# Row sums from accumulating exponentials: denominators folded into the softmax shift

## The reference

```python
def attention(q, k, v, wq, wk, wv, wo_w, wo_b):
    qp = rope(einsum('bsd,ed->bse', q, wq))
    kp = rope(einsum('bsd,ed->bse', k, wk))
    vp = einsum('bsd,ed->bse', v, wv)
    scores = einsum('bhnqd,bhnkd->bhnqk', qb, kband) * sqrt(32)
    scores = where(abs(k_pos - q_pos) <= 128, scores, neg)     # a band of keys
    out = einsum('bhnqk,bhnkd->bhnqd', softmax(scores, -1), vband)
    return einsum('bsd,ed->bse', out, wo_w) + wo_b

def ffn(x, W_in, b_in, W_out, b_out):                          # 8-bit weights, 16-bit activations, simulated
    hidden = gelu(quantize_a16(x) @ quantize_w8(W_in) + b_in)
    return quantize_a16(hidden) @ quantize_w8(W_out) + b_out

x = x + attention(layernorm(x), ctx, ctx, wq, wk, wv, wo_w, wo_b)
x = x + ffn(layernorm(x), W_in, b_in, W_out, b_out)
```

## Time and profile before

| | |
|---|---|
| median of 3 runs | 1174.8 us (1173.72 to 1175.84) |
| profiled execution | 1176.49 us, its span 1174.8 us |
| granted TensorE clock, mean | 0.988 |
| TensorE busy | 1135.5 us, 97% |
| VectorE busy | 946.8 us, 81% |
| ScalarE busy | 646.8 us, 55% |
| GpSimd busy | 375.7 us, 32% |

### The profile page before, as it was taken

The page is one execution under the profiler, slowest core; times in us unless marked ns, Lnnn a source line. Parts: engine busy times, 40 slices in busy tenths (PEclk is TensorE's granted clock), DMA queues, the critical chain, the costliest instruction groups (busy, mean ns, idle before and its releaser), DMA issues.

```text
span 1174.8 us, 23540 instructions
## 1 busy us (share of the span) xinstructions
PE 1135.5 (97%) x7928; PEld 766.9 (65%) x7928; DVE 946.8 (81%) x2413; ACT 646.8 (55%) x1033; POOL 375.7 (32%) x540
## 2 busy tenths in 40 slices
PE   6999999999999999999999789999999999999998
PEld 6867887887788788778878464444444444444443
DVE  6879989999999999999998756666666687777776
ACT  5255356436534643563464255555555577777774
POOL 1247337534743663474365230000000021111121
PEclk9989999999999999999999799999999999999999
DMA  8554674566457556646753723555553402676662
GB/s 281 133 150 114 172 221 118 148 184 163 126 175 212 129 137 184 172 123 179 203 139 92 222 65 118 197 196 198 196 196 117 152 1 77 214 232 227 224 216 99
DMA packets 100522, 191.10 MB, mean 163 GB/s; under 512 B 13376, under 2 KB 30912, under 8 KB 100416
## 3 DMA queue, kind: packets, MB, share of 16 engines
q1 hardware_dynamic: 96096, 179.92, 50.9%
q10 hardware_dynamic: 4320, 9.83, 2.8%
HBM read 89.16 MB, written 43.91 MB: 113 GB/s over the span
## 4 chain that ended last, share of the span: by engine, by line
PE 44%; DVE 26%; issue 25%; DMA 2%; ACT 1%; SPq 1%; DVEq 0%; POOL 0%; POOLq 0%; ACTq 0%
PE bank L864 19%; DVE bank L1224 12%; PE bank L642 6%; PE bank L656 5%; PE bank L669 5%; DVE row_max L1224 3%; PE bank L589 3%; PE bank L593 2%; DVE neg_max L1265 2%; DVE roped L1250 2%; DVE rt L1248 2%; DVE rt L1247 1%; DVE neg_max L1229 1%; DVE t_lo L1257 1%; PE bank L608 1%
## 5 line engine op out<-in xcount | busy, mean ns | idle before, releaser
L1224 DVE CUSTOM_DVE_ANT_0 bank<-bank,mask 128x256 f32<-128x256 f32 x512 | 203.5, 453 | 33.9 <-PE bank L608 23.1
L864 PE MATMUL bank<-wout_int,g_hi 128*128 128x512 bf16 x512 | 193.6, 379 | 0.1
L864 PE MATMUL bank<-wout_int,g_lo 128*128 128x512 bf16 x512 | 193.6, 379 | 0.0
L825 PE MATMUL bank<-qT_hi,win_int 128*128 128x512 bf16 x496 | 188.0, 379 | 0.0
L825 PE MATMUL bank<-qT_lo,win_int 128*128 128x512 bf16 x496 | 188.0, 379 | 0.0
L973 ACT ACTIVATE probs<-bank 128x512 f32<-128x512 f32 x256 | 139.0, 599 | 37.0 <-PE bank L642 31.1
L1542 POOL TENSOR_TENSOR k_lo<-roped,k_hi 128x256 fp32r<-128x256 f32 x60 | 55.0, 947 | 263.5 <-ACT k_hi L913 263.5
L1520 DVE TENSOR_TENSOR g_lo<-h_int,g_hi 128x512 f16<-128x512 f32 x128 | 89.1, 696 | 41.3 <-ACT g_hi L1129 37.4
L1565 POOL TENSOR_SCALAR_AFFINE_SELECT probs<-probs 128x256 f32<-128x256 f32 x256 | 107.1, 429 | 35.9 <-ACT probs L973 30.0
L1097 ACT ACTIVATE h_ring<-bank,b_in,g_scale 128x512 f32<-128x512 f32 x96 | 73.1, 779 | 71.2 <-PE bank L825 56.4
L1462 DVE TENSOR_REDUCE hmax<-h_ring 128x512 f32 (+1 forms) x96 | 63.1, 682 | 58.5 <-ACT h_ring L1097 56.4
(11 more groups left out here) (170 smaller groups left out, 2735.0 us busy)
## 6 DMA issues: line engine op xcount, KB each, us to landing
hidden_scratch<-h_ring SPq DMA_DIRECT2D x96, 256.0 KB, 2.1
h_ring<-hidden_scratch SPq DMA_DIRECT2D x96, 256.0 KB, 2.9
k_st<-k_hi SPq DMA_DIRECT2D x128, 128.0 KB, 2.9
q_st<-q_hi SPq DMA_DIRECT2D x128, 128.0 KB, 2.7
xq<-x_scratch SPq DMA_DIRECT2D x16, 1024.0 KB, 6.0
x_ln<-in_x SPq DMA_DIRECT2D x16, 512.0 KB, 6.3
ctx_raw<-in_ctxT SPq DMA_DIRECT2D x16, 512.0 KB, 5.0
k_st<-k_lo SPq DMA_DIRECT2D x64, 128.0 KB, 2.8
```

The source lines that it names most:

```text
L825: mm = pe.matmul(bank[f % 4][:], win_int[:, c, f * P:(f + 1) * P], part[:, par, c], start=c == 0 and part is qT_hi, stop=c == KC - 1 and p ...
L864: return pe.matmul(bank[4 * par + u][:], part[:, f % 4, u * P:(u + 1) * P], wout_int[:, f], start=f == 0 and part is g_hi, stop=f == FC - ...
L1224: dve.tensor_tensor_reduce(sc, sc, mask[:, (1 - qb) * P:(1 - qb) * P + S], 1.0, NEG, ALU.add, ALU.max, row_max[:, qb, n:n + 1]).then_inc(m ...
```

## The change

Scores come out negated: `wq` is scaled by -sqrt(32) when it is split (`wq_scaled`, `wq_rest`), so VectorE takes row minima, and the masked entries are a large positive number. In the first half ScalarE takes, after VectorE's minimum of a head, the exponential of the masked scores in place, with the minimum as bias, and accumulates its row sum: two instructions of 128x256 per head (`row_sums`). After head 15, ScalarE computes the logarithm of all sums and the exponential of its negation (`logs`), and VectorE combines minimum, logarithm and one correction step into the shift rows (`log_sums`, five instructions). With these, the exponential of the second half gives normalised probabilities. The denominators, their inversion, the DMAs, `normalise` and the `pick` matmuls are gone.

A score bank is now free when the sums have read it. Heads 12 and 15 use a third bank (6). The k cast moves from ScalarE to GpSimd (`k_lead`), the ctx cast from ahead of the exponentials to behind the fifth, and GpSimd's four `ctx_lo` to behind bands 10 to 13. Twelve output products stand before the shift transposes, where there were seven.

```diff
-            def row_maxima(b, n):
+            def row_minima(b, n):
                 dve.wait_ge(s_mm, H * b + n + 1)
                 apart(dve)
                 for qb in range(2):
-                    sc = ring[n % 2][:, qb * S:(qb + 1) * S]
-                    dve.tensor_tensor_reduce(sc, sc, mask[...], 1.0, NEG, ALU.add, ALU.max, row_max[:, qb, n:n + 1]).then_inc(max_done, 1)
+                    sc = early[n][:, qb * S:(qb + 1) * S]
+                    dve.tensor_tensor_reduce(sc, sc, mask[...], 1.0, FAR, ALU.add, ALU.min, row_min[:, qb, n:n + 1]).then_inc(min_done, 1)
...
+            def row_sums(b, n):
+                if n == 0:
+                    wait(act, lse_chain, LSE_OPS * b)
+                act.wait_ge(min_done, 2 * (H * b + n + 1))
+                for qb in range(2):
+                    sc = early[n][:, qb * S:(qb + 1) * S]
+                    act.activation(sc, sc, ACT.Exp, scale=-1.0, bias=row_min[:, qb, n:n + 1],
+                                   accum_out=row_sum[:, qb, n:n + 1]).then_inc(sum_done, 1)
+
+            def logs(b):
+                act.wait_ge(sum_done, 2 * H * (b + 1))
+                act.activation(lse[:], row_sum[:], ACT.Ln).then_inc(log_done, 1)
+                act.wait_ge(log_done, 2 * b + 1)
+                act.activation(lse_e[:], lse[:], ACT.Exp, scale=-1.0).then_inc(log_done, 1)
...
+            def log_sums(b):
+                hi, lo = shift[:, :, MROW:MROW + H], shift[:, :, MROW + H:P]
+                link = chain(dve, lse_chain, LSE_OPS * b)
+                dve.wait_ge(log_done, 2 * b + 1)
+                link(dve.tensor_tensor(lse_z[:], lse[:], row_min[:], ALU.subtract))
+                dve.wait_ge(log_done, 2 * b + 2)
+                link(dve.tensor_tensor(lse_t[:], row_sum[:], lse_e[:], ALU.mult))
+                link(dve.scalar_tensor_tensor(out=lse_z[:], in0=lse_t[:], scalar=-1.0, in1=lse_z[:], op0=ALU.add, op1=ALU.add))
+                link(dve.tensor_copy(hi.bitcast(F32R), lse_z[:]))
+                link(dve.tensor_tensor(lo.bitcast(F32R), lse_z[:], hi, ALU.subtract))
...
+        early = [bank[i] for i in (0, 1, 0, 1, 0, 1, 0, 1, 0, 1, 0, 1, 6, 0, 1, 6)]
+        ahead = [max([m for m in range(n) if early[m] is early[n]], default=None) for n in range(H)]
...
-            def scores(b, n):
+            def scores(b, n, has_proj):
                 if n < 2:
                     wait(pe, exp_done, H * b)
+                elif ahead[n] is not None:
+                    pe.wait_ge(sum_done, 2 * (H * b + ahead[n] + 1))
+                elif has_proj:
+                    pe.wait_ge(v_done, 2 * (b + 2) - 1)
                 else:
-                    pe.wait_ge(max_done, 2 * (H * b + n - 1))
+                    wait(pe, oT_out, 2 * b - 1)
...
             def clump(b, par, i, has_proj):
                 for kb in range(2):
-                    weighted(b, par, i, kb)
-                for kb in range(2):
-                    denominators(b, i, kb, has_proj)
+                    weighted(b, par, i, kb, has_proj)
...
-                some(7)
+                some(12)
                 max_transposes(b, has_proj)
                 some(4)
-                for n, count in enumerate((1, 2, 2, 2, 1, 1, 1, 0, 1, 1, 0, 0, 1, 0, 0, 0)):
+                for n, count in enumerate((1, 1, 1, 1, 1, 0, 1, 0, 1, 0, 0, 0, 1, 0, 0, 0)):
...
             def ot_lead(j, s, has_q):
-                act.wait_ge(onorm, 2 * (j + 1) if j < NB - 1 else 2 * j + s + 1)
+                act.wait_ge(oT_out, 2 * (j + 1))
...
+            def k_lead(j):
+                pool.wait_ge(rope_step["k"], ROPE_OPS * (j + 1))
+                for i in range(NC4):
+                    wait(pool, stacked["k"][i], STAGED * j)
+                pool.tensor_copy(part_hi["k"][:], roped[:]).then_inc(hi_done["k"], 1)
...
                 for n in range(H):
                     band(b, n)
                     if 6 <= n < 10 and has_proj:
                         split_lo("q", b + 1, n - 6)
-                    if n in (1, 3) and has_xt:
-                        ctx_lo(b + 2, n // 2 + 2)
+                    if 10 <= n < 14 and has_xt:
+                        ctx_lo(b + 2, n - 10)
```

More of the change, by code:

```diff
@@ L40 @@
 SLOTS = 8
-HOT = DK + NC4 - 1
 FC = FF // P
@@ L74, in constants @@
     q, k = np.arange(S)[:, None], np.arange(S)[None, :]
-    mask = folded(folded(np.where(np.abs(q - k) <= WINDOW, 0.0, NEG).astype(np.float32), 0), 1)
+    mask = folded(folded(np.where(np.abs(q - k) <= WINDOW, 0.0, FAR).astype(np.float32), 0), 1)
     assert not mask[:P, :P].any() and not mask[P:, P:].any()
     mask = np.concatenate([mask[P:], mask[:P, P:]], 1)
-    hot = np.tile((np.arange(HOT) % NC4 == NC4 - 1).astype(np.float32), (P, 1))
-    row, col = np.arange(P)[:, None], np.arange(P)[None, :]
-    pick = np.stack([row == DK * (col // DK) + i for i in range(NC4)], 1).astype(np.float32)
     sel = np.zeros((P, H), np.float32)
@@ L563, in qk_tile @@
                     pe.wait_ge(xt_lo, 2 * j + 2)
-                else:
-                    wait(pe, den_done, j - 1)
                 dst = (kv_bank if which == "k" else q_bank)[half]
@@ L644, in scores_t, with weighted @@
                 mm.then_inc(st_mm, 1)
-            def weighted(b, par, i, kb):
+            def weighted(b, par, i, kb, has_proj):
                 if kb == 0:
@@ L652, in weighted @@
                     elif i == 2:
-                        pe.wait_ge(mT_done, MAX_COPIES * (b + 1))
+                        if has_proj:
+                            pe.wait_ge(v_done, 2 * (b + 2))
+                        else:
+                            pe.wait_ge(oT_out, 2 * b)
                 for c in range(KC):
@@ L659, in weighted @@
                     mm.then_inc(pv_mm, 1)
-            def denominators(b, i, kb, has_proj):
-                if i == 0 and kb == 0:
-                    wait(pe, den_done, b)
-                    if has_proj:
-                        pe.wait_ge(rope_step["q"], ROPE_OPS * (b + 2))
-                one_hot = hot[:, NC4 - 1 - i:NC4 - 1 - i + DK]
-                for c in range(KC):
-                    n = KC * i + c
-                    mm = pe.matmul(den_bank[DK * c:DK * (c + 1), 0:S], one_hot, probs[:, n % SLOTS, kb],
-                                   start=i == 0 and kb == 0, stop=i == NC4 - 1 and kb == 1)
-                if kb == 1:
-                    mm.then_inc(den_mm, 1)
             def clump(b, par, i, has_proj):
                 for kb in range(2):
-                    weighted(b, par, i, kb)
-                for kb in range(2):
-                    denominators(b, i, kb, has_proj)
+                    weighted(b, par, i, kb, has_proj)
             def w_transposes(b, has_proj):
@@ L761, in _ @@
             steps(pe, step)
-            def last_shares():
-                pe.wait_ge(pick_in, 16)
-                pe.wait_ge(exp_done, H * NB)
-                for s in range(2):
-                    pe.wait_ge(den_done, NB + s)
-                    for i in range(NC4):
-                        mm = pe.matmul(ring[s][:, i * P:(i + 1) * P], pick[:, i], den_r[:, s * P:(s + 1) * P],
-                                       start=True, stop=True)
-                    mm.then_inc(share_mm, 1)
             def last_products():
@@ L1043, in step @@
                     softmax_exp(b, n)
+                    if n == 4 and has_xt:
+                        ctx_hi(b + 2)
                     if n == 6 and has_proj:
```

144 lines of the change are left out of this document (54 added, 90 removed).

## The result

The changed kernel takes 1310.9 us (median of 4 runs, 1309.8 to 1312.6) against 1175.3 us for the kernel before on the same chip: a ratio of 1.116, 95% interval 1.114 to 1.118. Forecast were 1260 us, with a range up to 1305. The direction held, and so did most of the walk through the queues; 51 us were missing. The profiled execution has a span of 1310.9 us against 1174.8.

What follows compares the result with a forecast made beforehand. TensorE was taken as the bound, VectorE close behind in the first half. Steps of 29.1 + 17.8 = 46.9 us against 40.8, +6.1 x 15 = 91, less 6, gave +85: 1260 us; own range 1230 to 1300, wider range 1190 to 1305.

Steps and rivals of the forecast that it cites:

- the clock falls: Rival: holes in the second half lower TensorE's clock, +4 us a step, about 1320 us; chance 0.05.
- The price of a sum: ScalarE, first half: 0.42 us per accumulating exponential, 0.36 plus 0.06 for writing out the sum; ends 0.36 and 0.60.
- The other estimate in the forecast: From the Trainium skill: 0.40 us for a 256-element exponential with bias, without the accumulator; time about 10 us above forecast.
- dear: Rival: the accumulator costs 0.60 us or more a sum on ScalarE in the first half, 1308 us; chance 0.13.
- The first half: Forward scores to shift transposes: 24.3 us of TensorE work plus 4.8 of stalls, 29.1 instead of 24.2.
- The hold: Log chain ending the first half: GpSimd's bias addition holds one small VectorE operation, charged 0.9 us.
- The listed stalls: TensorE's first-half waits before scores 2, 3, 6, 7, 9, 11 and the shift transposes, given as 4.8 us.
- The second half: From the shift transposes: GpSimd's late ctx_lo decides, last band at 16.7, end at 17.8 us instead of 16.6.
- TensorE keeps its gain: First rival: TensorE stays the bound, a step is 39.3 to 39.6 us, 1151 us; chance 0.12.
- the second rival: Only GpSimd's late ctx_lo costs: first half 24.3, second 17.8, +1.3 us a step, 1188 us; chance 0.10.
- Alone that would be 52 us: TensorE sheds four clumps of denominators, 3.4 us a step on the path, over 15 steps.
- The last step: First half some 22 us as before, second 3.4 less, about 3 less behind it; together -6 us.

Runs made afterwards that it cites:

- the filling: Changed kernel with idle bf16 matmuls (15 and 19) in TensorE's two holes before the third and fourth clump, steps 0 to 13: 1287.0 us, ratio 1.096.
- the run without reads: Changed kernel with the filling, its 32 exponentials a step kept but without the accumulated sum: 1273.7 us, ratio 1.085.
- the run without sums: Changed kernel with the filling, without the 32 first-half exponentials and sums; a score bank is free after its minima: 1192.2 us, ratio 1.016.
- the early ctx: Changed kernel with the ctx cast back ahead of the exponentials, GpSimd's four ctx_lo back before band 0 and after bands 1 and 3: 1275.8 us, ratio 1.085.
- VectorE lightened: Kernel before without denominators, reciprocals and products, and three VectorE quantisation operations cut from 512 to 32 columns: 1142.5 us, ratio 0.972.
- A third bank: Changed kernel with the filling and a third score bank for nearly all heads: 1271.5 us, ratio 1.083.

## Why the prediction was wrong

The failed step is the one on the clock: the forecast added nothing for it, and it cost about 34 of the 51 us that were missing. The walk of the queues held; its first half was 1.2 us too short.

- *The clock.* The forecast kept TensorE at full speed and gave "the clock falls" 0.05, at +4 a step. It fell, to 0.92 over the steps, and the holes that the forecast itself had found (1.7 and 2.3 us forecast, 1.6 and 2.1 measured) are the ones that had to be filled to bring it back to 0.98. Price by the filling: 26 us shown, some 8 more by the same rate, an estimate: about 34. It was less than the rival's 60, which put all 11 us of the second half's work at half speed: 120 us at the lower level are 8 a step, in which at most 4 us of work can be lost, and 2.3 showed. The last step in the earlier trace rows, with its granted 0.65, said what holes do.
- *The price of a sum.* 0.42 forecast, 0.45 measured. The exponential was right at 0.36; the read adds 0.09, not 0.06. By the run without reads, in proportion, that is 0.4 us a step, 6 us. The other estimate in the forecast, 0.40 for the exponential alone, was 0.04 too high. The accumulator was not "dear" (0.60).
- *The first half*, 29.1 forecast, 30.3 at full clock. The hold was there with its size (1.0 for 0.9). Scores 3, 7, 9 and 11 waited for the sums as walked, but the last sums ended at 27.6 and not 26.7, and the log chain took 2.7, not 2.4. Term by term: TensorE's own work is 24.7 us by the run without sums (24.3 forecast), the ring delays the last scores by 3.5 (2.9), and the hole before the shift transposes is 2.15 (1.8). The listed stalls add up to 4.7 and not 4.8, a slip of 0.1. With the sum's price these 1.2 us a step are 18 us.
- *The second half*, 17.8 forecast, 17.82 measured at full clock. GpSimd's late ctx_lo decided it as walked; with the early ctx it is 14.5 in the step where the clock stays up. That the shift rows' DMA leaves a wait held too, and GpSimd's k cast (1.04 us, not 1.6 to 2.6) cost nothing, as in the forecast.
- *TensorE keeps its gain* was no case: with the sums gone and GpSimd as changed, the kernel is still 1.6% slower, which is the second rival's 1188 (1192 measured). And without any sums or denominators, a step of the kernel before gains 0.9 us and not 3.4, so "Alone that would be 52 us" was wrong. VectorE was part of it, with 1.1 us to give; with VectorE lightened the gain is 1.6 us a step, and the DMA of q_lo and GpSimd's bands stand next.
- *The range.* It ended at 1305, while two of the forecast's own rivals, with 0.18 between them, stood at 1308 and 1320. So it left out not their far end but their values.
- *The last step.* I had its first half at 22 us, it took 25.8 at a granted 0.54; the part behind it fell by 4.9 us. Net 1 us instead of 6.

The terms make 56 for the 51 missed: 34 for the clock, 18 for the first half, 5 for the last step, less 1.4 at the start. The sum took fifteen full steps, and two aren't full. The first half of the first step takes 28.3 us instead of 30.3 even in the filled kernel, and the second half of the fifteenth, which has no ctx_lo left, 14.7 instead of 17.85.

Several expectations of the experiments missed in one and the same way: effects were added that share one chain. Output products ahead of the shift transposes looked like 2.8 us of extra path, but are cover for the log chain as soon as the sums are gone. And the filling was taken to be free, where in two runs it stood on the path.

## What to carry to other kernels

Before booking what an engine sheds, read the slack of the one behind it where the two meet: VectorE was idle for 1.1 us at the step's border, and of 3.4 us off TensorE 0.9 came out. An engine put into a buffer ring costs in three places: by the turns of the ring, by its other work, which now comes late, and as a tail behind the last buffer. A third bank mended only the first, 1.3 of 5.6 us. When a walk of the queues leaves TensorE with holes of about 2 us in every step, ask for its clock in the trace, and when a run with something left out is to price anything else, fill those holes first. Then look again: the filling must not stand ahead of the work it waits beside, and the clock of the two kernels must agree.

## What the hardware showed that I had not expected

- The accumulator's output on ScalarE is an instruction of its own (206 ns mean) that overlaps the next one: sums start 0.45 us apart, the same exponentials without it 0.36.
- The stretches at the lower clock are short and come right behind holes. One of them made a second half 18.9 us instead of 17.85; over the steps some 91 us at half the clock cost 26.
- Leaving work out lowered the clock: without the reads the steps were granted 0.90 instead of 0.92, and a gain of 13 us showed as 4. With the two holes filled it still fell, from 0.98 to 0.97 without the reads and to 0.96 with three banks.
- Beside GpSimd, VectorE operations stretch by far more than their own length: a 128x32 product took 1.19 us instead of 0.19 beside an addition, and a 128x512 one 2.85 beside six bands, where it took 0.49 to 1.41 in the kernel with the early ctx alone.
